# Score blocks of an attention unit set between the matmuls of an up tile, in an mLSTM attention and FP4 FFN kernel

## The chip, the cores and the metric

The kernel runs on one core of one Trainium2 chip. The metric is the device time in microseconds (us) of one execution, the median of several. Names of engines are those of the profile: PE is the matmul engine (TensorE), PEld its weight loads, DVE is VectorE, ACT is ScalarE, POOL is GpSimd, SP is the engine that issues the transfers.

## What is computed

Two residual layers over `x` of 8 x 256 x 512. The first is an mLSTM attention with 16 heads of 32 elements, whose queries are the normalised `x` and whose keys and values are `ctx`. The second is a gated FFN with FP4 weights, inner width 1408.

```python
qk = jnp.einsum('bhsd,bhtd->bhst', qh, kh) / jnp.sqrt(dh)      # heads of 32
C = qk * D                                                      # D: decay matrix, from the gates
Cn = C / (jnp.maximum(jnp.abs(C.sum(-1, keepdims=True)), jnp.exp(-max_log_D)) + EPS)
h = jnp.einsum('bhst,bhtd->bhsd', Cn, vh)                       # then normalised per head
...
gate_up = jnp.einsum('bsh,oh->bso', x, w_gu)                    # w_gu = FP4 value * scale of 128 inputs
h = jax.nn.silu(gate) * up
y = jnp.einsum('bsi,hi->bsh', h, w_down)
...
x = x + _L0_xattn_ref(_layernorm(x), ctx, ctx, ...)
x = x + _L0_ffn_ref(_layernorm(x), ...)
```

## The kernel before

**Tiling.** The batch is taken in four pairs of sequences (512 tokens). Each pair first goes through the attention and then through the FFN. The function `iteration(p, q, n)` runs the attention of pair p beside the FFN of pair q = p - 1, and prepares pair n = p + 1. So the program has five stages: attention of pair 0 alone; attention 1 beside FFN 0; attention 2 beside FFN 1; attention 3 beside FFN 2; FFN 3 alone. The change touches the three in the middle.

**The attention of a pair** is cut into 8 units `u`, each with four heads of one sequence. A sequence of 256 tokens is two blocks of 128. For a unit PE computes:

- the scores (`scores`, L883): eight f32 products of 32 x 128 by 32 x 128, four for the even heads (`hh` = 0) and four for the odd ones (`hh` = 1). Two of them, `half` 0 and 1, use different 32 rows of the array and stand side by side. An f32 matmul is two instructions (two passes) with a weight load each;
- the state sums (`state_sums`, L895), one f32 product over all 128 rows, which needs `vw` from POOL (L505). In the program they stand between the two calls of `scores`;
- the values (`values_up`, L943): eight f32 products of 33 columns, and at their end one product with the state (L948) that releases DVE's `later` (L1214) and ACT's `tok` (L671).

**The FFN of a pair** has 22 up tiles `h` of 128 outputs. Each is four groups `g` (128 inputs each, with a scale of their own), and a group is two f16 matmuls of 128 x 512 (`up_group`, L1013), parts 0 and 1. The four groups use four PSUM banks, `pf` 0 to 3. ACT takes groups 0 and 1 out of the bank (`ts`, L698), DVE groups 2 and 3 (L1296, L1300). An up tile's group g may begin when group g of the tile before has been taken out.

**The order on PE** is written out by hand. With u = 1 to 7 one round of two up tiles reads: the odd tile, with a value product in front of each of its eight matmuls (`values_up`), then the state product L948, then `scores` of the next unit for `hh` = 0, `state_sums`, `scores` for `hh` = 1, then the even tile's eight matmuls in a row (`ffn_up`). In the stage with FFN 0 all unit work stands two tiles later (`LATE`).

**The order on DVE** in that round: L1296 and L1300 of the even tile, (in the stage with FFN 0 also L1364, a piece of the down weights), `later` L1214, L1296 and L1300 of the odd tile, then the two `products` L1201 (they wait for `qk_done`, which the last score matmul raises), `state` L1206, `gate` L1309, `add_later` L1224, and again L1296 and L1300 of the even tile. An engine takes its instructions in order, so the even tile's L1296 and L1300 are queued behind the products of the unit.

**POOL** in that round: two sums L535, the product `hT` L540 (waits for DVE's gate), the two masks L494, the two `vw` L505.

Of the kernel before, what the change touches and what calls it, by code (L numbers as in the profile page):

```python
# [32 lines left out]
P = 128  # L33
B, S, E, NH = 8, 256, 512, 16
DH = E // NH
PAIRS = B // 2
TT = 2 * S // P
KT = E // P
# [10 lines left out]
BLKS = 2  # L49
# [16 lines left out]
SCORES = {h: u for u, h in enumerate(SCORES_AT)}  # L66
# [43 lines left out]
def xattn_ffn(nc, x, ctx, ctxT, w_gates, b_gates, ln_scale, gu_bytes, gu_scales, dn_bytes, dn_scales, out):  # L110
# [7 lines left out]
    with es:  # L118
# [22 lines left out]
        xT = sb("xT", [P, 2 * KT, TT * P])  # L141
# [55 lines left out]
        po = es.enter_context(nc.psum_tensor("po", [P, 512], F32))  # L197
# [8 lines left out]
        def slot(q, h):  # L206

            return h - LATE if q == 0 else h
# [9 lines left out]
        def bank_qk(p, u, half):  # L218
            return pf[:, 2 * half] if p == 0 and u % 2 else pq[:, 2 * half]
# [52 lines left out]
        qk_half = sem("qk_half")  # L272
# [539 lines left out]
        def _(pe):  # L812
# [42 lines left out]
                last = pe.transpose(bank_back(p)[:, 8 * DH:8 * DH + ROWS], lf[:, 0, P:S], ident[0:ROWS, 0:ROWS])  # L855
                last.then_inc(back_done, 1)

            def scores(p, q, u, hh):
                hg, b = u // 2, u % 2
                if p == 0 and u == 1 and hh == 0:  # L860

                    pe.wait_ge(floor_ready, 2)
                if p > 0 and u == 0 and hh == 0:

                    pe.wait_ge(floor_ready, 2 * p + 2)
                if hh == 0:
                    pe.wait_ge(xT_read, KT * p + hg + 1)
                    if p == 0:
                        if u > 1:
                            pe.wait_ge(prod_done, 2 * u - 2)  # L870
                    elif u > 0:
                        pe.wait_ge(prod_done, 2 * UNITS * p + 2 * u)
                    elif q is not None:
                        pe.wait_ge(t_ready, 4 * FT * q + 1)
                        pe.wait_ge(acc_ready, 4 * FT * q + 1)
                else:
                    pe.wait_ge(qk_half, UNITS * p + u + 1)
                for blk in range(BLKS):
                    t0 = b * S + blk * P
                    for half in range(2):  # L880
                        r = slice((2 * half + hh) * DH, (2 * half + hh + 1) * DH)
                        c = (blk * 2 + hh) * P
                        last = pe.matmul(bank_qk(p, u, half)[:, c:c + P], xT[r, KT + hg, t0:t0 + P],  # L883
                                         xT[r, hg, t0:t0 + P], start=True, stop=True)
                last.then_inc(qk_done if hh else qk_half, 1)

            def state_sums(p, q, u):

                hg, b = u // 2, u % 2
                pe.wait_ge(vw_ready, 2 * UNITS * p + 2 * u + 2)  # L890
                if u > 0:
                    pe.wait_ge(later_ready, UNITS * p + u)
                elif q is not None:
                    pe.wait_ge(t_ready, 4 * FT * q + 2)
                pe.matmul(pq[:, 1, 0:HG * (DH + 1)], ctx_sb[:, 2 * b, hg * P:(hg + 1) * P],  # L895
                          vw[:, u % 2].rearrange("q h d -> q (h d)"), start=True, stop=True
                          ).then_inc(st_done, 1)
# [28 lines left out]
            def values_up(p, q, u, h):  # L926
                hg, b = u // 2, u % 2
                if u == 0 and q is not None:
                    pe.wait_ge(acc_ready, 4 * FT * q + 2)
                if p == 0 and u < 2:  # L930
                    pe.wait_ge(v_ready, 2 * u + 2)
                elif u == 0:
                    pe.wait_ge(v_ready, TT * p + TT)
                if u > 0:
                    pe.wait_ge(o_read, UNITS * p + u)
                elif not (isinstance(p, int) and p == 0):
                    pe.wait_ge(o_read, UNITS * p)
                for k in range(2 * HG):
                    half, blk, hh = k // HG, k // 2 % 2, k % 2
                    if k % HG == 0:  # L940
                        pe.wait_ge(prod_done, 2 * UNITS * p + 2 * u + 1 + half)
                    col = (blk * HG + 2 * half + hh) * (DH + 1)
                    pe.matmul(po[:, col:col + DH + 1], dmat[:, u % 2, half, blk, hh],  # L943
                              v_sb[:, 2 * b + blk, hg * HG + 2 * half + hh], start=True, stop=True)
                    up_group(q, h, k // 2, k % 2)

                pe.wait_ge(state_ready, UNITS * p + u + 1)
                pe.matmul(pq[:, 1, HG * (DH + 1):2 * HG * (DH + 1)], xT[:, hg, b * S + P:(b + 1) * S],  # L948
                          state[:, u % 2].rearrange("q h d -> q (h d)"), start=True, stop=True
                          ).then_inc(pv_done, 1)  # L950
# [48 lines left out]
            def up_group(q, h, g, part):  # L999

                prev = behind(q, h)
                if part == 0:
                    if spare(q, h) and (prev < 0 or not spare(q, prev)):
                        pass
                    elif prev < 0 or spare(q, prev) != spare(q, h):

                        if q > 0:
                            pe.wait_ge(y_scaled, TT * (q - 1) + g + 1)
                    elif g < 2:
                        pe.wait_ge(t_ready, 4 * FT * q + 2 * prev + 1 + g)  # L1010
                    else:
                        pe.wait_ge(acc_ready, 4 * FT * q + 2 * prev - 1 + g)
                ins = pe.matmul(bank(q, h, g), gu_val[:, h // 2 + h % 2 * FT, g], yT[:, part, g],  # L1013
                                start=(part == 0), stop=(part == 1))
                if part == 1:
                    ins.then_inc(pu_done, 1)
# [26 lines left out]
            def keep_busy(count, dst=None):  # L1043

                words = ident[:].bitcast(F16)
                for _ in range(count):
                    pe.matmul(pf[:, 3] if dst is None else dst, words[:, 0:P], words.unsqueeze(1).to_broadcast([P, 2, 2 * P]),  # L1047
                              start=True, stop=True)

            def iteration(p, q, n):  # L1050
                for h in range(GU):
                    if q is not None:
                        if p is not None and slot(q, h - 1) in VALUES:
                            values_up(p, q, VALUES[slot(q, h - 1)], h)
                        else:
                            ffn_up(q, h)
                    if p is not None:

                        s = slot(q, h)
                        if q is None and s in VALUES and VALUES[s] + 1 < UNITS:  # L1060
                            scores(p, q, VALUES[s] + 1, 0)
                            if VALUES[s] == 0:
                                keep_busy(6, po[:])
                            else:
                                keep_busy(3)
                        if q is None and s in VALUES:
                            values(p, q, VALUES[s])
                            if q is None and VALUES[s] + 1 < UNITS:
                                scores(p, q, VALUES[s] + 1, 1)
                                state_sums(p, q, VALUES[s] + 1)  # L1070
                                keep_busy(6 if VALUES[s] == 0 else 3)
                        if s in SCORES and (q is not None or SCORES[s] == 0):
                            scores(p, q, SCORES[s], 0)
                            if q is None:
                                keep_busy(8, po[:])
                            state_sums(p, q, SCORES[s])
                            scores(p, q, SCORES[s], 1)
                if q is not None:
                    down(q, 0, range(FT))
                    down(q, 1, range(FT))  # L1080
                if n is not None:
                    if q is None:
                        keep_busy(16)
                    turn_x(n)
                    gate_sums(n)
                    if q is None:
                        keep_busy(36)
                if q is not None:
                    down(q, 2, range(FT))
                if p is not None:  # L1090
                    turn_y(p)
                if q is not None:
                    down(q, 3, range(FT - 3))
                if n is not None:
                    turn_back(n)
                if q is not None:
                    down(q, 3, range(FT - 3, FT))
# [387 lines left out]
```

## Time and profile before

| | us |
|---|---|
| median of 3 runs | 537.66 |
| the runs | 537.6 to 538.22 |
| time of the profiled execution | 538.07 |
| its span, first to last instruction | 536.4 |
| PE busy | 492.7 |
| DVE busy | 390.9 |
| POOL busy | 332.8 |
| ACT busy | 295.1 |

The span is what the trace covers, and 1.7 us of the execution lie around it. In the trace a line of several instructions of a kind is merged: its start is that of the first, its length reaches to the end of the last, and xN is their number. A matmul's end is modelled, so the distance from start to start is what a matmul costs in a row of them. The time in square brackets is how long the engine was idle ahead of the line, and what released it.

### The profile page before, as it was taken

How to read it: one execution, taken by the hardware profiler on the slowest of the kernel's cores; microseconds unless marked ns; L12 is line 12 of the kernel's file. 1: busy time of each engine (PE TensorE's matmuls, PEld its weight loads, DVE VectorE, ACT ScalarE, POOL GpSimd, SP SyncE). 2: the span in 40 equal slices, each digit the busy share in tenths (PEclk: the TensorE clock that was granted, in tenths of full speed). 3: DMA queues.
4: the chain of work that ended last, by engine and by line, in shares of the span. 5: the costliest groups of instructions: out<-in, count | busy, mean ns of one | idle time of the engine just before them, and what ended most of it. 6: DMA issues, size and time to landing. Idle time of an engine off the chain costs nothing.

```text
span 536.4 us, 8218 instructions
## 1 busy us (share of the span) xinstructions
PE 492.7 (92%) x2752; PEld 284.4 (53%) x2752; DVE 390.9 (73%) x691; ACT 295.1 (55%) x639; POOL 332.8 (62%) x371
## 2 busy tenths in 40 slices
PE   0989996899999899999999999999999989989996
PEld 0556773437777344567774445577764443323442
DVE  4976878978898988278878997478879754777301
ACT  0356854387877342688877334788863125765010
POOL 2064546188887764568887883678879644888401
PEclk9988997999999999999999999999999999999999
DMA  8964037074103200366015001671000010200001
GB/s 273 253 208 148 3 107 266 16 265 156 41 2 133 104 0 2 107 214 232 0 41 198 0 1 42 203 270 40 1 1 1 20 40 20 79 0 1 21 20 39
DMA packets 22235, 47.81 MB, mean 89 GB/s; under 512 B 1841, under 2 KB 8881, under 8 KB 21681
## 3 DMA queue, kind: packets, MB, share of 16 engines
q1 hardware_dynamic: 22192, 47.28, 25.7%
q8 instruction: 22, 0.36, 0.3%
q14 instruction: 21, 0.16, 0.1%
HBM read 37.31 MB, written 4.33 MB: 78 GB/s over the span
## 4 chain that ended last, share of the span: by engine, by line
PE 63%; DVE 16%; POOL 7%; issue 6%; ACT 5%; DMA 1%; DVEq 0%; POOLq 0%; ACTq 0%
PE pf L1028 26%; PE pf L1013 14%; PE pq L883 6%; PE po L943 4%; PE pq L895 3%; POOL dmat L494 3%; POOL hT L540 2%; PE pq L1013 2%; PE po L917 2%; PE pf L1047 2%; DVE ffn L1296 2%; DVE dmat L1201 2%; ACT dmat L664 2%; DVE th L1309 1%; PE pq L842 1%
## 5 line engine op out<-in xcount | busy, mean ns | idle before, releaser
L1013 PE MATMUL pf<-yT,gu_val 128*128 128x512 f16 x552 | 158.7, 381 | 5.6 <-DVE ffn L1300 2.4
L1028 PE MATMUL pf<-w_down,hT 128*128 128x512 f32 x352 | 154.0, 595 | 1.7 <-DVE w_down L1364 1.7
L535 POOL TENSOR_TENSOR ffn<-ffn,ts 128x512 f32<-128x512 f32 x88 | 118.2, 1346 | 28.0 <-DVE ffn L1300 21.1
L1028 PEld LDWEIGHTS pf<-w_down,hT 128*128 128x128 f32 x352 | 65.9, 190 | 83.7 <-issue 77.2
L698 ACT ACTIVATE ts<-pf,gu_scale 128x512 f32<-128x512 f32 x138 | 86.9, 682 | 17.1 <-PE pf L1013 15.9
L1013 PEld LDWEIGHTS pf<-yT,gu_val 128*128 128x128 f16 x552 | 62.7, 121 | 52.2 <-DVE ffn L1300 8.9
L664 ACT ACTIVATE dmat<-negm,aT 128x128 f32<-128x128 f32 x248 | 77.6, 393 | 0.5 <-DMA negm<-negm_dram 0.5
L943 PEld LDWEIGHTS po<-v_sb,dmat 128*128 128x128 f32 x384 | 66.2, 191 | 8.0
L540 POOL TENSOR_TENSOR hT<-ffn,th 128x512 f32<-128x512 f32 x44 | 57.7, 1316 | 19.9 <-DVE th L1309 19.9
L494 POOL TENSOR_SCALAR_AFFINE_SELECT dmat<-dmat 128x512 f32<-128x512 f32 x64 | 44.2, 706 | 27.1 <-ACT dmat L664 27.1
L1296 DVE SCALAR_TENSOR_TENSOR ffn<-pf,gu_scale,ts 128x512 f32<-128x512 f32 x69 | 51.4, 745 | 12.7 <-ACT ts L698 12.1
L1300 DVE SCALAR_TENSOR_TENSOR ffn<-pf,gu_scale,ffn 128x512 f32<-128x512 f32 x69 | 51.8, 751 | 9.0 <-PE pf L1013 1.4
L943 PE MATMUL po<-v_sb,dmat 128*128 128x33 f32 x384 | 58.4, 234 | 0.0
L716 ACT ACTIVATE th<-pf 128x512 f32<-128x512 f32 x16 | 9.5, 592 | 72.7 <-PE pf L1028 72.7
L546 POOL TENSOR_SCALAR ms<-ssq 128x1 f32<-128x1 f32 x16 | 4.2, 260 | 61.1 <-ACT th L716 60.6
L883 PE MATMUL pq<-xT 32*128 32x128 f32 x448 | 40.9, 301 | 0.0
L1201 DVE SCALAR_TENSOR_TENSOR dmat<-pq,dmat 128x512 f32<-128x512 f32 x56 | 36.1, 686 | 6.4 <-PE pq L883 6.2
L484 POOL TENSOR_TENSOR v_sb<-ctx_sb,vmean 128x512 f32<-128x512 f32 x16 | 16.8, 1079 | 29.8 <-DVE negm L1186 18.5
L883 PEld LDWEIGHTS pq<-xT 32*128 32x128 f32 x448 | 30.0, 189 | 9.4 <-issue 3.3
L1309 DVE SCALAR_TENSOR_TENSOR th<-th,ffn 128x512 f32<-128x512 f32 x44 | 34.1, 782 | 0.0
L1013 PE MATMUL pq<-yT,gu_val 128*128 128x512 f16 x114 | 30.2, 393 | 2.3 <-issue 2.1
L707 ACT ACTIVATE th<-ffn 128x512 f32<-128x512 f32 x44 | 27.5, 626 | 8.1 <-POOL ffn L535 8.1
(128 smaller groups left out, 678.7 us busy)
## 6 DMA issues: line engine op xcount, KB each, us to landing
negm<-negm_dram SPq DMA_DIRECT2D x31, 512.0 KB, 5.6
ffn<-in_x SPq DMA_DIRECT2D x4, 1024.0 KB, 6.7
xT<-in_ctx_T SPq DMA_DIRECT2D x16, 256.0 KB, 5.8
ctx_sb<-in_ctx SPq DMA_DIRECT2D x4, 1024.0 KB, 5.4
x_sb<-in_x SPq DMA_DIRECT2D x4, 1024.0 KB, 5.3
x_res<-x_sb SPq DMA_DIRECT2D x4, 1024.0 KB, 4.7
out<-x_res SPq DMA_DIRECT2D x16, 256.0 KB, 2.1
ts<-in_gate_up_bytes SPq DMA_DIRECT2D x4, 352.0 KB, 9.3
```

The costliest lines, as they stand in the source:

```text
L494: pool.affine_select(out=d, in_=d, compare_op=ALU.is_ge, fill=0.0, base=0, pattern=[[0, HG], [1, P]], channel_multiplier=-1).then_inc(mask ...
L535: pool.tensor_tensor(acc, acc, ts[:, h % TDEEP, 1], ALU.add).then_inc(tsum_ready, 1)
L540: pool.tensor_tensor(hT[:, j], ffn[:, 6 + j % 2], th[:, j % 2], ALU.mult).then_inc(h_ready, 1)
L664: last = act.activation(dmat[:, u % 2, half, c, hh], m[:, c * P:(c + 1) * P], ACT.Exp, bias=aT[:, c, bh:bh + 1])
L698: act.activation(ts[:, h % TDEEP, g], bank(q, h, g), ACT.Copy, scale=gu_scale[:, g * GU + o:g * GU + o + 1]).then_inc(t_ready, 1)
L883: last = pe.matmul(bank_qk(p, u, half)[:, c:c + P], xT[r, KT + hg, t0:t0 + P], xT[r, hg, t0:t0 + P], start=True, stop=True)
L943: pe.matmul(po[:, col:col + DH + 1], dmat[:, u % 2, half, blk, hh], v_sb[:, 2 * b + blk, hg * HG + 2 * half + hh], start=True, stop=True)
L1013: ins = pe.matmul(bank(q, h, g), gu_val[:, h // 2 + h % 2 * FT, g], yT[:, part, g], start=(part == 0), stop=(part == 1))
L1028: last = pe.matmul(pf[:, tt], hT[:, j, tt * P:(tt + 1) * P], w_down[:, j], start=(j == 0), stop=(j == FT - 1))
L1201: dve.scalar_tensor_tensor(d, bank_qk(p, u, half), float(DH) ** -0.5, d, ALU.mult, ALU.mult).then_inc(prod_done, 1)
L1296: dve.scalar_tensor_tensor(acc, bank(q, h, 2), gu_scale[:, 2 * GU + o:2 * GU + o + 1], ts[:, h % TDEEP, 0], ALU.mult, ALU.add).then_inc(ac ...
L1300: dve.scalar_tensor_tensor(acc, bank(q, h, 3), gu_scale[:, 3 * GU + o:3 * GU + o + 1], acc, ALU.mult, ALU.add).then_inc(acc_ready, 1)
```

## The change

`scores` is split into its waits (`scores_free`) and its blocks (`score_block`, L886), and a new function `scores_up` puts the blocks of a unit, the state sums and the even up tile into one order. In front of each of the first four matmuls of the tile (groups 0 and 1, both parts) stands one score block, that is two products side by side; the state sums stand in the middle. Groups 2 and 3 follow in a row. The matmuls, their operands, the banks and the semaphores are the same; the stage without FFN keeps its order.

```diff
+            def scores_up(p, q, u, h):
+
+                scores_free(p, q, u, 0)
+                for blk in range(BLKS):
+                    score_block(p, u, 0, blk)
+                    up_group(q, h, 0, blk)
+                state_sums(p, q, u)
+                scores_free(p, q, u, 1)
+                for blk in range(BLKS):
+                    score_block(p, u, 1, blk)
+                    up_group(q, h, 1, blk)
+                for g in range(2, KT):
+                    up_group(q, h, g, 0)
+                    up_group(q, h, g, 1)
...
                         if p is not None and slot(q, h - 1) in VALUES:
                             values_up(p, q, VALUES[slot(q, h - 1)], h)
+                        elif p is not None and slot(q, h - 1) in SCORES:
+                            scores_up(p, q, SCORES[slot(q, h - 1)], h)
                         else:
                             ffn_up(q, h)
...
-                        if s in SCORES and (q is not None or SCORES[s] == 0):
+                        if q is None and s in SCORES and SCORES[s] == 0:
                             scores(p, q, SCORES[s], 0)
-                            if q is None:
-                                keep_busy(8, po[:])
+                            keep_busy(8, po[:])
                             state_sums(p, q, SCORES[s])
                             scores(p, q, SCORES[s], 1)
```

The order of instructions on PE, in a unit with u from 1 to 7 beside the FFN. `pq<-xT` is a score product, `pq<-vw,ctx_sb` the state sums, `pf<-yT,gu_val` a matmul of the up tile. Before:

```order
180 L883 MATMUL pq<-xT 128x128 [waits prod_done,xT_read]
181 L883 MATMUL pq<-xT 128x128 x3
182 L895 MATMUL pq<-vw,ctx_sb 128x132 [waits later_ready,vw_ready]
183 L883 MATMUL pq<-xT 128x128 [waits qk_half]
184 L883 MATMUL pq<-xT 128x128 x3
185 L1013 MATMUL pf<-yT,gu_val 128x512 [waits t_ready]
186 L1013 MATMUL pf<-yT,gu_val 128x512
187 L1013 MATMUL pf<-yT,gu_val 128x512 [waits t_ready]
188 L1013 MATMUL pf<-yT,gu_val 128x512
189 L1013 MATMUL pf<-yT,gu_val 128x512 [waits acc_ready]
```

The same place after the change:

```order
182 L886 MATMUL pq<-xT 128x128 [waits prod_done,xT_read]
183 L886 MATMUL pq<-xT 128x128
184 L1037 MATMUL pf<-yT,gu_val 128x512 [waits t_ready]
185 L886 MATMUL pq<-xT 128x128 x2
186 L1037 MATMUL pf<-yT,gu_val 128x512
187 L919 MATMUL pq<-vw,ctx_sb 128x132 [waits later_ready,vw_ready]
188 L886 MATMUL pq<-xT 128x128 [waits qk_half]
189 L886 MATMUL pq<-xT 128x128
190 L1037 MATMUL pf<-yT,gu_val 128x512 [waits t_ready]
191 L886 MATMUL pq<-xT 128x128 x2
192 L1037 MATMUL pf<-yT,gu_val 128x512
193 L1037 MATMUL pf<-yT,gu_val 128x512 [waits acc_ready]
```

Four matmuls of the up tile moved in between the score products: two ahead of the state sums, one between the last two pairs of score products, one behind them.

The order on PE at the first unit (u = 0) of a stage, where the scores follow the second up tile and not a tile with values. Before:

```order
149 L1013 MATMUL pf<-yT,gu_val 128x512
150 L883 MATMUL pq<-xT 128x128 [waits t_ready,acc_ready,xT_read,floor_ready]
151 L883 MATMUL pq<-xT 128x128 x3
152 L895 MATMUL pq<-vw,ctx_sb 128x132 [waits t_ready,vw_ready]
153 L883 MATMUL pq<-xT 128x128 [waits qk_half]
154 L883 MATMUL pq<-xT 128x128 x3
155 L1013 MATMUL pf<-yT,gu_val 128x512 [waits t_ready]
```

The same place after the change:

```order
149 L1037 MATMUL pf<-yT,gu_val 128x512
150 L886 MATMUL pq<-xT 128x128 [waits t_ready,acc_ready,xT_read,floor_ready]
151 L886 MATMUL pq<-xT 128x128
152 L1037 MATMUL pf<-yT,gu_val 128x512 [waits t_ready]
153 L886 MATMUL pq<-xT 128x128 x2
154 L1037 MATMUL pf<-yT,gu_val 128x512
155 L919 MATMUL pq<-vw,ctx_sb 128x132 [waits t_ready,vw_ready]
156 L886 MATMUL pq<-xT 128x128 [waits qk_half]
```

The same matmuls moved here. The order on DVE, ACT, POOL and SP is that of before.

## Rows read from the trace of the kernel before

**Rows 1.** The page, section 2: granted clock in 40 slices, in tenths.

```profile
PEclk9988997999999999999999999999999999999999
```

**Rows 2.** Busy time by stretch: PE, PEld, DVE, ACT, POOL, clock, DMA, in stages 2, 3.

```profile
117.50:173.40 55.90, 54.34 (x418) 41.23 (x418) 49.40 (x86) 43.25 (x105) 47.00 (x54) 1.00 0.24 83
230.40:283.70 53.30, 53.30 (x414) 40.69 (x414) 42.17 (x77) 43.21 (x104) 41.78 (x53) 1.00 0.35 125
```

**Rows 3.** Timeline of PE in the third stage, one round: start, length, line, count.

```profile
256.59 0.38 PE L1013 MATMUL pf<-yT,gu_val 128*128 128x512 f16 x1
256.81 0.39 PE L948 MATMUL pq<-state,xT 128*128 128x132 f32 x2
257.13 0.71 PE L883 MATMUL pq<-xT 32*128 32x128 f32 x8
257.77 0.49 PE L895 MATMUL pq<-vw,ctx_sb 128*128 128x132 f32 x2
258.19 0.71 PE L883 MATMUL pq<-xT 32*128 32x128 f32 x8
258.84 1.90 PE L1013 MATMUL pf<-yT,gu_val 128*128 128x512 f16 x8
...
262.16 0.38 PE L1013 MATMUL pf<-yT,gu_val 128*128 128x512 f16 x1
...
262.94 0.39 PE L1013 MATMUL pf<-yT,gu_val 128*128 128x512 f16 x1
...
263.53 0.39 PE L948 MATMUL pq<-state,xT 128*128 128x132 f32 x2
```

**Rows 4.** Timeline of DVE in the same round.

```profile
257.24 0.30 DVE L1214 TENSOR_TENSOR later<-pq,decay 128x132 f32<-128x132 f32 x1 [1.07 <-PE pq L948]
...
258.30 0.75 DVE L1300 SCALAR_TENSOR_TENSOR ffn<-pf,gu_scale,ffn 128x512 f32<-128x512 f32 x1
259.06 1.29 DVE L1201 SCALAR_TENSOR_TENSOR dmat<-pq,dmat 128x512 f32<-128x512 f32 x2
...
262.13 0.75 DVE L1300 SCALAR_TENSOR_TENSOR ffn<-pf,gu_scale,ffn 128x512 f32<-128x512 f32 x1
```

**Rows 5.** PE timeline, windows so narrow that first and last score passes stand alone.

```profile
257.13 0.38 PE L883 MATMUL pq<-xT 32*128 32x128 f32 x2
...
257.56 0.28 PE L883 MATMUL pq<-xT 32*128 32x128 f32 x2
...
258.63 0.28 PE L883 MATMUL pq<-xT 32*128 32x128 f32 x2
258.84 0.39 PE L1013 MATMUL pf<-yT,gu_val 128*128 128x512 f16 x1
```

**Rows 6.** PE timeline, narrow window: f16 matmul, then score products (first unit, second stage).

```profile
117.17 0.38 PE L1013 MATMUL pf<-yT,gu_val 128*128 128x512 f16 x1
117.48 0.38 PE L883 MATMUL pq<-xT 32*128 32x128 f32 x2
```

**Rows 7.** PE timeline, first stage: score passes, then a filler matmul without a wait.

```profile
60.02 0.39 PE L883 MATMUL pf<-xT 32*128 32x128 f32 x4
60.34 0.60 PE L1047 MATMUL pf<-ident 128*128 128x512 f16 x2
```

**Rows 8.** Timeline of PE, second stage, one round.

```profile
138.00 0.39 PE L948 MATMUL pq<-state,xT 128*128 128x132 f32 x2
...
139.24 0.49 PE L895 MATMUL pq<-vw,ctx_sb 128*128 128x132 f32 x2 [0.21 <-POOL vw L505]
139.66 0.71 PE L883 MATMUL pq<-xT 32*128 32x128 f32 x8
145.00 0.39 PE L948 MATMUL pq<-state,xT 128*128 128x132 f32 x2
...
146.24 0.49 PE L895 MATMUL pq<-vw,ctx_sb 128*128 128x132 f32 x2 [0.21 <-POOL vw L505]
```

**Rows 9.** Timeline of DVE, then of POOL, in the same round.

```profile
140.53 1.29 DVE L1201 SCALAR_TENSOR_TENSOR dmat<-pq,dmat 128x512 f32<-128x512 f32 x2 [0.30 <-PE pq L883]
...
143.60 0.75 DVE L1300 SCALAR_TENSOR_TENSOR ffn<-pf,gu_scale,ffn 128x512 f32<-128x512 f32 x1
...
145.63 0.55 POOL L505 TENSOR_TENSOR vw<-v_sb,dmat 128x66 f32<-128x66 f32 x2
```

**Rows 10.** Timeline of DVE at the first unit of the fourth stage.

```profile
345.11 1.29 DVE L1201 SCALAR_TENSOR_TENSOR dmat<-pq,dmat 128x512 f32<-128x512 f32 x2 [0.31 <-PE pq L883]
...
347.72 0.75 DVE L1300 SCALAR_TENSOR_TENSOR ffn<-pf,gu_scale,ffn 128x512 f32<-128x512 f32 x1 [0.46 <-PE pf L1013]
```

More of the change, by code:

```diff
@@ L856, in turn_back, with scores_free @@
                 last.then_inc(back_done, 1)
-            def scores(p, q, u, hh):
-                hg, b = u // 2, u % 2
+            def scores_free(p, q, u, hh):
+                hg = u // 2
                 if p == 0 and u == 1 and hh == 0:
@@ L877, in scores, with score_block @@
                     pe.wait_ge(qk_half, UNITS * p + u + 1)
-                for blk in range(BLKS):
[L879 to L885, printed above, removed]
+            def score_block(p, u, hh, blk):
+                hg, b = u // 2, u % 2
+                t0 = b * S + blk * P
+                for half in range(2):
+                    r = slice((2 * half + hh) * DH, (2 * half + hh + 1) * DH)
+                    c = (blk * 2 + hh) * P
+                    last = pe.matmul(bank_qk(p, u, half)[:, c:c + P], xT[r, KT + hg, t0:t0 + P],
+                                     xT[r, hg, t0:t0 + P], start=True, stop=True)
+                if blk == BLKS - 1:
+                    last.then_inc(qk_done if hh else qk_half, 1)
+            def scores(p, q, u, hh):
+                scores_free(p, q, u, hh)
+                for blk in range(BLKS):
+                    score_block(p, u, hh, blk)
+            def scores_up(p, q, u, h):
[11 more added lines that the diff above has]
+                    up_group(q, h, g, 1)
             def state_sums(p, q, u):
```

## The prediction

> **What bounds the kernel now.** I read the granted clock first: from the second stage on it is full [rows 1], and it is 1.00, the 2.4 GHz level, in both stretches of units that I priced [rows 2]. Then the busy time by stretch: in the third stage PE is busy for all 53.30 us, in the second for 54.34 of 55.90 [rows 2]. That looks like a kernel bound by PE, and the change as one that can give PE something. But a busy PE is not a PE that streams, since a matmul that waits for its weights counts as busy. So I went to single starts.
>
> A round in the third stage, from one state product L948 to the next, is 263.53 - 256.81 = 6.72 us [rows 3]. Within it PE has a small hole: the matmuls of groups 2 and 3 of the odd tile start at 262.16 and 262.94, 0.78 apart, where 0.72 (two value products and two f16 matmuls) would do. The even tile's L1300 on DVE ends at 262.13 + 0.75 = 262.88 [rows 4], and the matmul that needs its bank starts 0.06 later. So a **loop through DVE** is already tight: L948 starts; 2.25 later the products start (259.06); 3.82 later L1300 of the even tile ends (262.88), with no idle time in between; 0.06 later PE goes on; 0.59 later L948 starts. 2.25 + 3.82 + 0.06 + 0.59 = 6.72, the whole round. What starts the products at 259.06? Two things at once: L1300 of the odd tile ends at 258.30 + 0.75 = 259.05, and the last pass of the scores starts at 258.63 [rows 5]. In the second stage, where DVE does wait for the scores, the products start at 140.53, and the last pass there starts 0.44 after 139.66 [rows 8, 9], so the scores' last start and DVE are 0.43 apart; 258.63 + 0.43 = 259.06. Both are just in time.
>
> In the second stage a round is 145.00 - 138.00 = 7.00 us [rows 8]. There PE waits for POOL's `vw` at the state sums (0.21 idle), and the loop runs state sums, scores, products, gate, hT, masks, vw: 146.24 - 139.24 = 7.00. The DVE loop is slack in that stage by 0.28.
>
> **The price of a switch between 32 rows and 128 rows.** This decides the case. The steps, start to start:
> - In a run of score passes: 257.13 to 257.56 is three steps, 0.43. The first passes last 0.38 and later ones 0.28 [rows 5], so the first waits 0.10 longer for its weights: the steps are 0.21, 0.11, 0.11.
> - Scores to f16: 258.63 to 258.84, 0.21 [rows 5]. The pass itself takes 0.11, so 0.10 is lost. It is not the semaphore wait on that matmul: in the first stage a filler matmul without any wait also starts 0.32 after two passes of 60.02, so 0.21 after the last [rows 7].
> - f16 to scores: 117.17 to 117.48, 0.31 [rows 6], against 0.22 from an f16 matmul to the full-row L948 [rows 3]; 0.09 is lost, and the score pass again lasts 0.38, so its weights were not loaded under the f16 matmul: a further 0.10.
> - L948 to scores: the scores start 0.32 after L948 and L948's second pass 0.11 after its first, so 0.21: 0.10 lost, and again a 0.38 pass. Scores to state sums is 0.21 (257.56 to 257.77) [rows 3, 5]; from there to the next scores it is 0.42, of which 0.21 is such a step, so the state sums' two passes are 0.21 apart where 0.11 would do.
>
> So each step into the 32-row form costs 0.20, and each step out 0.10 and its exposed load (0.01 for f16, 0.11 for f32).
>
> **The change on PE.** Before, a unit has four such switches. After, eight: L948 to scores, out and in around three f16 matmuls, out to the fourth, and in again behind the state sums; only the step from f16 to state sums is a cheap one. I count from the start of L948. Before: scores 0.32, last pass 1.82, first f16 2.03, group 2 of the even tile at 2.03 + 0.23 + 3 x 0.215 = 2.90. After: scores 0.32; second pass 0.53; f16 0.74; scores +0.32 = 1.06; 1.27; f16 1.48; state sums +0.23 = 1.71; second pass 1.82; scores 2.03; 2.24; f16 2.45; scores 2.77; last pass 2.98; f16 3.19; group 2 at 3.42. PE's own stream grows by 3.42 - 2.90 = **0.52** a unit, and the last pass of the scores moves from 1.82 to 2.98, **1.16** later: it now has three f16 matmuls ahead of it besides.
>
> **The change on DVE.** It issues nothing new, but its products wait for that last pass: they start at 2.98 + 0.43 = 3.41 and not at 2.25. Queued behind them are the state copy, the gate, the late sum, and L1296 and L1300 of the even tile, for which PE waits in the odd tile. The round becomes 3.41 + 3.82 + 0.06 + 0.59 = 7.88, 1.16 more than 6.72. PE's own stream would be 6.72 + 0.52 = 7.24 less its 0.06 hole, so PE is to stand idle for some 0.6 a round where the groups 2 and 3 of the odd tile want their banks.
>
> ACT and POOL: groups 0 and 1 of the even tile now end early and far apart, which ACT can only use; POOL's hT, masks and vw follow the gate and are done 5.71 after the products start (140.53 to 146.24), while PE reaches its next state sums 3.82 + 0.65 + 1.71 = 6.18 after them. So vw is no longer waited for, and I cost both at nothing; if that cover of 0.47 went, it would be a longer round still. No transfer is moved.
>
> **The sum.** Third and fourth stage: 7 rounds of 1.16. The first unit has no gate and no late sum behind its products, and there DVE waited 0.31 ahead of the products and again 0.46 for PE ahead of L1300 [rows 10]; with that slack DVE's part of the shift, 1.16 - 0.46 = 0.70 less what PE waits for it anyway, comes out near PE's own, and I take PE's 0.52. That gives 2 x (7 x 1.16 + 0.52) = 17.3 for the two stages. Second stage: the DVE loop there is 3.41 + 3.82 (140.53 to 143.60 + 0.75) + 0.65 (144.35 to 145.00) = 7.88 against 7.00, so 7 x 0.88, and 1.16 for the first unit, since DVE has the gate behind its products already: 7.3. The first and last stage are as they were. Together 24.6. On the profiled execution's 538.07 that is 562.7, on the median of 537.66 it is **562.2 us**.
>
> **Rules that speak for and against.** The row-to-full switch without a wait [rows 7] is dear by 0.10. The Trainium skill, TensorEngine Tiling (Array Packing), section Tiling Modes, says that a change of tiling mode drains the array, without a price; by it each of the added switches costs something, the sum stays as it is, and the trace agrees with 0.10. The Trainium skill, TensorE: Matmul & The Clock Gate, Part 2: What happens when you issue a matmul, says that weight loads are pulled ahead of running matmuls when they go to the background buffer. By that rule alone the score weights would come in under the f16 matmuls and the time would be that of rival 2; the trace disagrees, with 0.38 for the pass behind an f16 matmul [rows 6].
>
> **Rivals.**
> 1. *PE's stream alone.* If DVE catches up (its chain shortened by a different overlap, or PE's wait on L1300 not in the way), only 0.52 x 24 = 12.5 is paid: 550.2. Against it: the round of 6.72 closes through DVE to 0.01. Chance 0.12.
> 2. *The interleaving works as in the value tiles:* no drain, loads hidden. Then seven score passes of 0.11, three f16 matmuls of 0.22, L948 and the state sums of 0.22 each lie ahead of the scores' last pass: 0.77 + 0.66 + 0.44 = 1.87 against 1.82 before; PE's stream shrinks by about 0.7 (four switches and their loads), but DVE's loop sets the round and stays at 6.72 to 6.77. In the second stage the state sums to last pass is 0.88 against 0.86. So 0 to 24 x 0.05 = 1.2: 537.7 to 538.9, the case that is **not slower**. It decides when rows of 0.38 behind an f16 matmul become 0.28 and the 0.31 becomes 0.22. Chance 0.09, as [rows 6] show the opposite at just such a place. A version in which only the two loads behind f16 matmuls are hidden takes 0.2 from each 1.16: 24.6 - 24 x 0.2 = 19.8, 557.5; that lies within my forecast's own range.
> 3. *A further loop opens,* POOL's or ACT's: the first of the two products is done 3.41 + 0.65 = 4.06 after L948, and the value matmuls want it at 3.42 + 4 x 0.215 = 4.28 less a load of 0.1, a margin of about 0.1. With 0.2 a unit more it is 567; the same place is where a fall of the clock to its lower level would start, as PE now idles in each round (in the second stage it idled 0.21 a round and kept 1.00 [rows 2, 8]). Chance 0.07 above 567.
>
> **How the numbers follow.** The forecast, 555 to 567, has 0.72; rival 1 0.12, rival 2 0.09, rival 3 0.07. The range reaches down to rival 1, 549, and up to 567, and leaves out rivals 2 and 3. About 0.2% is what a measurement here can tell from no change, 1.1 us: rival 2 is mostly within it, so the chances are 0.02 faster, 0.08 same, 0.90 slower.
>
> **What would show it.** Right: rounds of about 7.9 in all three stages, score lines of x4 with length 0.5 and a first pass of 0.38, f16 to scores 0.31, the products L1201 idle by about 1.1 ahead of each and released by PE's score line, and PE's odd-tile matmuls waiting for L1300 and L1296. vw no longer in PE's waits. Rival 1: rounds of 7.2 with DVE idle. Rival 2: passes of 0.28 and rounds of 6.7. I am wrong as a whole if the switch costs less between single pairs than at the places where I read it.

## The result, and the profile after

The changed kernel took **562.24 us** (median of 4 runs, 561.86 to 564.24) against 537.94 for the kernel before beside it: 1.045 times as long, 95% interval 1.042 to 1.047. The forecast was 562.2, range 549 to 567. The profiled execution's span grew from 536.4 to 560.1 us.

The granted clock, section 2 of the page of after; nothing changed there in the stages with units [rows 1]:

```profile
PEclk9979997899999999999999999999999999999999
```

The page's section 5, groups of after: name, shapes, count, busy time and mean of one, then the idle time ahead and its main releaser.

```profile
L1226 DVE SCALAR_TENSOR_TENSOR dmat<-pq,dmat 128x512 f32<-128x512 f32 x56 | 36.1, 686 | 33.0 <-PE pq L886 33.0
...
L886 PE MATMUL pq<-xT 32*128 32x128 f32 x448 | 53.8, 323 | 0.0
```

DVE's products had 6.4 us of idle time ahead of them and now have 33.0, all put down to PE's scores. The score matmuls are as many as before and their mean grew from 301 to 323 ns: more of them are first passes, with the wait for weights in their length.

One round on PE in the third stage (timeline of after), the answer to [rows 3]:

```profile
267.25 0.39 PE L972 MATMUL pq<-state,xT 128*128 128x132 f32 x2
267.57 0.49 PE L886 MATMUL pq<-xT 32*128 32x128 f32 x4
267.99 0.39 PE L1037 MATMUL pf<-yT,gu_val 128*128 128x512 f16 x1
268.31 0.49 PE L886 MATMUL pq<-xT 32*128 32x128 f32 x4
268.73 0.39 PE L1037 MATMUL pf<-yT,gu_val 128*128 128x512 f16 x1
268.96 0.39 PE L919 MATMUL pq<-vw,ctx_sb 128*128 128x132 f32 x2
269.28 0.49 PE L886 MATMUL pq<-xT 32*128 32x128 f32 x4
269.70 0.39 PE L1037 MATMUL pf<-yT,gu_val 128*128 128x512 f16 x1
270.02 0.49 PE L886 MATMUL pq<-xT 32*128 32x128 f32 x4
270.44 1.25 PE L1037 MATMUL pf<-yT,gu_val 128*128 128x512 f16 x5
...
273.68 0.39 PE L1037 MATMUL pf<-yT,gu_val 128*128 128x512 f16 x1 [0.36 <-DVE ffn L1321]
...
275.13 0.39 PE L972 MATMUL pq<-state,xT 128*128 128x132 f32 x2
```

From L972 to L972 (L948 of before) it is 275.13 - 267.25 = 7.88 us. Where a score line stands next behind an f16 matmul, it starts 0.32 after it; the state sums start 0.23 after theirs. What follows a score line starts 0.42 after it. At 273.68 PE stands still for DVE. DVE in the same round, the answer to [rows 4]:

```profile
267.67 0.30 DVE L1239 TENSOR_TENSOR later<-pq,decay 128x132 f32<-128x132 f32 x1 [1.07 <-PE pq L972]
267.89 0.74 DVE L1321 SCALAR_TENSOR_TENSOR ffn<-pf,gu_scale,ts 128x512 f32<-128x512 f32 x1
...
268.73 0.75 DVE L1325 SCALAR_TENSOR_TENSOR ffn<-pf,gu_scale,ffn 128x512 f32<-128x512 f32 x1
...
270.66 1.29 DVE L1226 SCALAR_TENSOR_TENSOR dmat<-pq,dmat 128x512 f32<-128x512 f32 x2 [1.18 <-PE pq L886]
...
273.74 0.75 DVE L1325 SCALAR_TENSOR_TENSOR ffn<-pf,gu_scale,ffn 128x512 f32<-128x512 f32 x1
```

Products at 270.66, 3.41 after the state product; even tile's last accumulation done at 274.49, 3.83 after them; PE's next state product 0.64 later. The sum is 7.88.

**Where the time went,** from the starts of the matmuls in both traces:

| | before | after | difference |
|---|---|---|---|
| second stage: first scores to first state product | 6.44 | 7.48 | 1.04 |
| its seven rounds | 49.05 | 55.14 | 6.09 |
| third stage: the same | 6.32 | 6.88 | 0.56 |
| its seven rounds | 47.26 | 55.15 | 7.89 |
| fourth stage: the same | 6.32 | 7.10 | 0.78 |
| its seven rounds | 47.01 | 55.15 | 8.14 |
| last state product to first down matmul, three stages | 22.46 | 22.46 | 0.00 |

That is 24.5. The units of the second stage began 0.73 earlier in this execution of after (116.75 and 117.48), and 24.5 - 0.7 is the 23.7 between the spans within 0.1.

### The profile page after: what moved, and what is told of

Read it like the earlier page. It is cut to its first block, busy times and chain, and to the rows that moved or that the text cites. A ratio compares the mean times of both kernels' runs of the same rounds, so it can differ in the third digit from the quotient of the medians.

```text
span 560.1 us, 8218 instructions
## 1 busy us (share of the span) xinstructions
PE 511.2 (91%) x2752; PEld 288.2 (51%) x2752; DVE 390.7 (70%) x691; ACT 296.4 (53%) x639; POOL 332.0 (59%) x371
## 4 chain that ended last, share of the span: by engine, by line
PE 64%; DVE 17%; issue 8%; ACT 5%; POOL 4%; DMA 1%; DVEq 0%; POOLq 0%; ACTq 0%
PE pf L1052 25%; PE pf L1037 12%; PE pq L886 8%; DVE ffn L1321 4%; PE pf L1071 3%; DVE th L1334 3%; PE pq L842 2%; PE po L941 2%; PE po L967 2%; PE pq L1037 2%; PE pq L919 2%; DVE dmat L1226 1%; DVE tok L1249 1%; DVE ffn L1325 1%; ACT dmat L664 1%
## 5 line engine op out<-in xcount | busy, mean ns | idle before, releaser
L1037 PE MATMUL pf<-yT,gu_val 128*128 128x512 f16 x552 | 172.3, 383 | 13.5 <-DVE ffn L1321 8.4
L698 ACT ACTIVATE ts<-pf,gu_scale 128x512 f32<-128x512 f32 x138 | 89.8, 681 | 22.0 <-PE pf L1037 20.5
L1037 PEld LDWEIGHTS pf<-yT,gu_val 128*128 128x128 f16 x552 | 61.5, 119 | 64.0 <-DVE ffn L1321 15.0
L886 PE MATMUL pq<-xT 32*128 32x128 f32 x448 | 53.8, 323 | 0.0
L886 PEld LDWEIGHTS pq<-xT 32*128 32x128 f32 x448 | 33.7, 188 | 20.2 <-issue 14.2
L671 ACT ACTIVATE tok<-po 128x264 f32<-128x264 f32 x32 | 12.5, 390 | 44.5 <-PE pq L972 34.3
```

Source lines behind the costliest of these rows:

```text
L698: act.activation(ts[:, h % TDEEP, g], bank(q, h, g), ACT.Copy, scale=gu_scale[:, g * GU + o:g * GU + o + 1]).then_inc(t_ready, 1)
```

## The experiments

Each line of a diff is against the kernel that the text names; the label's expectation was written ahead of the run. The totals scatter by more than some of these edits are worth: the first stage, whose order is the same but for ACT's squares in the last three runs, ended (first scores of the second stage) anywhere from 115.4 to 119.8 us in the profiled executions. So what an edit costs is read from the rounds, and the totals stand beside them.

**Four switches, or eight.** The changed kernel with the four matmuls moved in twos:

```diff
-                scores_free(p, q, u, 0)
-                for blk in range(BLKS):
-                    score_block(p, u, 0, blk)
-                    up_group(q, h, 0, blk)
+                scores(p, q, u, 0)
+                up_group(q, h, 0, 0)
+                up_group(q, h, 0, 1)
                 state_sums(p, q, u)
...
+                scores(p, q, u, 1)
+                up_group(q, h, 1, 0)
+                up_group(q, h, 1, 1)
```

> The changed kernel with the same four matmuls of the even tile moved among the scores, but in twos: four score products, two matmuls, state sums, four score products, two matmuls. So a unit has four switches between 32 and 128 rows, as before the change, and not eight. My theory: PE's stream is 0.08 us a round shorter than before (the state sums' weights load under a matmul), but the scores' last pass stands 0.34 later, DVE's loop becomes 7.06: 14 rounds of 0.34 and a few tenths in the second stage, about 543 us. Rival (only PE's stream counts): 0.08 x 24 less than before, 536 us. Second rival (it is the moving of f16 matmuls among scores that costs, not the switch): near 562 us.

Measured: 544.46 us, 1.013 of before (1.009 to 1.018). Rounds were 7.05 in all three stages, 4.9 us more than before with the first units; the other 2.3 of the 7.2 between the spans lie ahead of the second stage. PE, then DVE, in one round of it:

```profile
253.53 0.39 PE L970 MATMUL pq<-state,xT 128*128 128x132 f32 x2
253.85 0.71 PE L886 MATMUL pq<-xT 32*128 32x128 f32 x8
254.50 0.60 PE L1035 MATMUL pf<-yT,gu_val 128*128 128x512 f16 x2
254.94 0.39 PE L917 MATMUL pq<-vw,ctx_sb 128*128 128x132 f32 x2
255.26 0.71 PE L886 MATMUL pq<-xT 32*128 32x128 f32 x8
...
259.14 0.39 PE L1035 MATMUL pf<-yT,gu_val 128*128 128x512 f16 x1 [0.19 <-DVE ffn L1319]
```

```profile
256.12 1.29 DVE L1224 SCALAR_TENSOR_TENSOR dmat<-pq,dmat 128x512 f32<-128x512 f32 x2 [0.36 <-PE pq L886]
```

The state sums' line is 0.39 long and no longer 0.49: I read that as its weights coming in under the f16 matmul. PE has no more switches than in the kernel before and this load less, and yet the round is 0.33 longer, because the products start 2.59 after the state product and not 2.25. So the delay of the last score pass costs by itself, without any added switch; and the same f16 matmuls among the scores cost 18 us less when they stand in twos.

**The switch alone.** The kernel before, with one small matmul added between the two blocks of each `scores` call, over 128 rows in one run and over 32 (`ident[0:DH]`) in the other:

```diff
+                if tile is not None:
+                    pe.wait_ge(t_ready, 4 * FT * q + 2 * (tile - 1) + 1)
                 for blk in range(BLKS):
+                    if blk == 1 and tile is not None:
+                        words = ident[0:P].bitcast(F16)
+                        pe.matmul(bank(q, tile, 0)[:, 0:DH], words[:, 0:P], words[:, 0:DH], start=True, stop=True)
                     t0 = b * S + blk * P
```

The added wait, for the bank that the small matmul writes, costs nothing: in both runs the scores start 0.32 after the state product, as in the kernel before.

> The kernel before, with one small f16 matmul over 128 rows and 32 columns added between the two score blocks of each call of the scores, two a unit, 48 in all; its result is overwritten. It adds switches and nothing else. My theory: 0.33 us for each, out 0.10, in 0.10, exposed score weights 0.10 and the matmul 0.03, so rounds of 6.72 + 0.66 = 7.38 and about 551.6 us. Rival (a switch costs nothing, the lost time is that of the f16 matmuls' length): 48 x 0.03 or less, 537 to 539 us.

> The same small matmul at the same 48 places, but over 32 rows, so that the array stays in its 32-row form. My theory: no switch, so only the matmul's own 0.03 to 0.06 us each, rounds of 6.8, 538 to 541 us. Rival (any foreign matmul between two score blocks costs, by its other type, bank or weights, whatever its rows): the same time as the one over 128 rows.

Measured: over 128 rows 551.97 us, 1.028 of before (1.022 to 1.033), rounds of 7.35; over 32 rows 540.33 us, 1.006 (1.004 to 1.008), rounds of 7.00, 6.82 and 6.82. PE in a unit of the 128-row run:

```profile
252.95 0.39 PE L953 MATMUL pq<-state,xT 128*128 128x132 f32 x2
253.27 0.49 PE L888 MATMUL pq<-xT 32*128 32x128 f32 x4
253.69 0.19 PE L883 MATMUL pf<-ident 128*128 128x32 f16 x1
253.81 0.49 PE L888 MATMUL pq<-xT 32*128 32x128 f32 x4
254.23 0.49 PE L900 MATMUL pq<-vw,ctx_sb 128*128 128x132 f32 x2
```

and of the 32-row run:

```profile
251.11 0.39 PE L953 MATMUL pq<-state,xT 128*128 128x132 f32 x2
251.43 0.49 PE L888 MATMUL pq<-xT 32*128 32x128 f32 x4
251.76 0.17 PE L883 MATMUL pf<-ident 32*128 32x32 f16 x1
251.76 0.48 PE L888 MATMUL pq<-xT 32*128 32x128 f32 x4
252.18 0.49 PE L900 MATMUL pq<-vw,ctx_sb 128*128 128x132 f32 x2
...
253.25 1.90 PE L1018 MATMUL pf<-yT,gu_val 128*128 128x512 f16 x8
```

From the first score line to the state sums is 0.96 in the one and 0.75 in the other, against 0.64 in the kernel before [rows 3]. The matmul over 128 rows costs 0.32, as added up from the steps; over 32 rows 0.11 here. The second small matmul of the unit, behind the state sums, costs nothing over 32 rows: from the state sums (252.18) to the first f16 matmul (253.25) it is 1.07, as in the kernel before [rows 3]. So the round grows by 0.10, from 6.72 to 6.82, and not by 0.22. Type, bank and weights are those of the same tile of numbers; the rows are what differs. With 32 rows the second stage kept its 7.00: there PE waits 0.21 for `vw` ahead of the state sums anyway, which takes up the 0.11, and the part behind them did not get longer.

**Is it PE's own stream or DVE's loop?** The changed kernel, with another order on DVE:

```diff
-                if u is not None:
-                    products(p, u, range(2))
-                    keep_state(p, u)
...
                         ffn_up(q, h, p, u)
+                        if h % 2 == 1 and h > 1:
+                            gate(q, h // 2 - 1)
+                        if u is not None:
+                            products(p, u, range(2))
+                        if p is not None and s in VALUES:
+                            keep_state(p, VALUES[s])
+                        if p is not None and s - 1 in ADD:
+                            add_later(p, ADD[s - 1])
                         if q == 0 and h % 2 == 0:
                             down_weights(h // 2)
-                        if h % 2 == 1 and h > 1:
-                            gate(q, h // 2 - 1)
...
-                    if p is not None and s in ADD:
+                    if q is None and s in ADD:
                         add_later(p, ADD[s])
```

> The changed kernel, with the DVE order of a round altered: the gate ahead of the two products, the state copy and the late sum behind the even tile's two accumulations. PE's order is that of the changed kernel. My theory (a round of 7.88 us closes through DVE: late last score pass, products, even tile's accumulations; PE's own stream is 7.24): DVE then needs 3.41 + 2.82 + 0.65 = 6.88 a round, so PE binds and rounds fall to about 7.24, in all 548 us. Rival (the added time is all PE's own, switches dearer than I priced them, and DVE only waits along): nothing changes, rounds of 7.88, 562 us.

Measured: 552.97 us, 1.029 of before (1.026 to 1.032). The rounds fell from 7.88 to 7.19 in all three stages, with PE's order untouched, so 0.69 of each was DVE's and not PE's. The total fell by 9 us only, not by 14: the ends of the stages, from the last state product to the first down matmul, grew from 6.28, 8.09 and 8.09 to 7.66, 9.88 and 9.87.

**What the same DVE order gives the kernel before.** With it alone, and with one f16 matmul between the first four score products and the state sums:

> The kernel before with the altered DVE order alone (gate ahead of the products, state copy and late sum behind the even tile's accumulations). My theory: in stages three and four the round of 6.72 us closes through DVE with a hole of 0.08 on PE, so PE's 6.64 becomes the round; in the second stage, where the loop ran over gate, hT, masks and vw, it falls from 7.00 to about 6.7. Together 3 to 3.5 us less, about 534.4 us. Rival (the kernel before is bound by PE): no change, 537.7 us.

> The altered DVE order, and one matmul of the even tile between the first four score products and the state sums, the other three behind the unit: four switches, the state sums' weights loaded under the matmul. My theory: PE's stream is 0.09 us a round shorter than in the kernel with the altered DVE order alone, 24 x 0.09 = 2.2 us, about 532.2 us. Rival (the state sums' second pass waits for something else than its weights): the time of the altered DVE order alone, or 0.2 us a unit more for a further delay of the scores.

Measured: 541.23 us, 1.005 (1.003 to 1.006), and 539.21 us, 1.001 (1.000 to 1.003). The rounds were as expected, 6.63 and 6.54, in all three stages (the last of the third excepted, 6.88 and 6.89); in the second stage alone the seven rounds of 6.63 are 2.6 us shorter than before. But both totals missed, by 7 us each. The stages' ends were 1.3, 1.8 and 1.7 us longer here too in the first of the two, and behind the second stage the clock was granted at its lower level for 3.4 us, which made the stretch from the first down matmul to the next scores 52.77 us and not 51.09. The end of the fourth stage in the first of the two:

```profile
404.25 0.95 DVE L1224 TENSOR_TENSOR tok<-tok,later 128x132 f32<-128x132 f32 x1
...
405.24 1.06 ACT L681 ACTIVATE dmat<-tok 128x1024 f32<-128x1024 f32 x1 [2.30 <-DVE tok L1224]
...
406.20 1.25 ACT L698 ACTIVATE ts<-pq,gu_scale 128x512 f32<-128x512 f32 x2
...
406.93 1.61 PE L1013 MATMUL pq<-yT,gu_val 128*128 128x512 f16 x6 [0.71 <-ACT ts L698]
```

ACT stands at its squares (L681) for 2.30 us, waiting for the late sum that my order had put later, and its copies of the next tile are queued behind, and PE behind those. I had costed the move of the late sum at nothing and had looked only at DVE.

**The late sum back in its place.** The two orders again with `add_later` straight behind the products:

> The kernel before with DVE's gate ahead of the two products and the state copy behind the even tile's accumulations; the late sum keeps its place. In the run before_dve_relieved the rounds were as short as expected (6.63), but ACT's squares at the end of a stage waited for the later late sum, and with them ACT's copies of the next tile. My theory: rounds of 6.63 again, the stages' ends as in the kernel before, so 14 x 0.09 + 7 x 0.37 = 3.8 us less, about 534 us. Rival (the lost time at the stages' ends comes from the gate or the state copy, or PE makes up for shorter rounds by waiting later): the 541 us of before_dve_relieved, or 537.7 us.

> The same DVE order, and one matmul of the even tile between the first four score products and the state sums (four switches a unit, the state sums' weights loaded under it). My theory: rounds of 6.54, stages' ends as before, 24 x 0.09 = 2.2 us less than gate_first, about 532 us, faster than both kernels of this case. Rival: the ends take it back as in one_matmul_between, 537 to 539 us.

> The changed kernel with the same DVE order. My theory: PE binds as in after_dve_relieved, rounds of 7.19, but the stages' ends stay at 6.3, 8.1 and 8.1 us as in the changed kernel, so 5 us less than the 553 us there: about 548 us. What is then left over the gate_first kernel, 14 us, is the price of the eight switches alone, 24 x 0.56. Rival: the ends are long because PE's rounds are shorter, 553 us.

Measured: 546.87 us, 1.014 (1.010 to 1.019); 543.50 us, 1.008 (1.005 to 1.011); 554.35 us, 1.029 (1.026 to 1.033), all slower than expected, by 13, 12 and 6 us. The ends were back at 6.28, 8.09 and 8.09, as expected, and the rounds were not: most took 7.52 and some 6.63 (6.54 in the second), 7.51 nearly throughout in the third. POOL and DVE in a round of 7.52 of the first:

```profile
404.74 1.27 POOL L540 TENSOR_TENSOR hT<-ffn,th 128x512 f32<-128x512 f32 x1
404.75 1.41 DVE L1224 TENSOR_TENSOR tok<-tok,later 128x132 f32<-128x132 f32 x1
```

The late sum, a sum of two operands in SBUF, takes 0.29 in a round of the kernel before and 1.41 here, started 0.01 behind POOL's hT; it ends 0.15 after hT. Of its 24 instances beside the FFN 21 took 1.36 to 1.41 us in this run, and 3 in the kernel before, all at a stage's end. The rounds of 6.63 are just those in which it took 0.28. The earlier gate had moved hT to just this moment. With the changed kernel's PE order (after_gate_first) the late sum started later within hT, took less, and again ended 0.15 after it:

```profile
266.98 1.28 POOL L540 TENSOR_TENSOR hT<-ffn,th 128x512 f32<-128x512 f32 x1
267.68 0.73 DVE L1249 TENSOR_TENSOR tok<-tok,later 128x132 f32<-128x132 f32 x1
```

The products there start 3.41 after the state product as in the changed kernel, so the longer late sum was enough to let DVE set the round again, 7.51 and not 7.19. The Trainium skill, SBUF — State Buffer, section SBUF: two separate sides, says that a VectorE operation with two SBUF inputs and a GpSimd operation that reads SBUF lock a shared port pair for their whole length and that the later one blocks; the trace agrees.

**Both mended.** The DVE order as in after_dve_relieved, with the late sum behind the accumulations, and ACT's squares one tile later:

```diff
-SQUARES = {SCORES_AT[-2] + 3: 0, SCORES_AT[-1] + 3: 1}
+SQUARES = {SCORES_AT[-2] + 4: 0, SCORES_AT[-1] + 4: 1}
```

> The kernel before_dve_relieved, with ACT's two squares at the end of a stage one tile later. There the rounds were 6.63 but ACT's copies of the next tile stood behind squares that waited for the late sum, 1.3 to 1.8 us a stage. In gate_first the late sum, put straight behind the products, took 1.40 us instead of 0.29 because POOL's hT had just started. My theory: the late sum takes 0.28 in the rounds, rounds of 6.63, the stages' ends 6.3 to 7.0, 8.1 to 8.9 and 8.1 to 8.9 us, about 535 us. Rival (the ends wait for DVE, not for ACT's squares): ends of 7.6, 9.9 and 9.8 us and 540 us again.

> The same with one matmul of the even tile between the first four score products and the state sums. My theory: rounds of 6.54, ends as in the kernel beside it, about 533 us, faster than both kernels of this case. Rival: 538 to 539 us, as one_matmul_between.

> The changed kernel's PE order with the same DVE and ACT order: PE binds, rounds of 7.19, and against the first kernel of this call only the eight switches a unit are left, 24 x 0.56 = 13.4 us more than that one, about 548 us. Rival (part of the change's cost is neither PE's switches nor DVE's wait): more than 15 us above that one.

Measured: 535.37 us, **0.994 of before** (0.992 to 0.996); 534.81 us, **0.993** (0.991 to 0.996); and with the changed kernel's PE order 548.66 us, 1.019 (1.015 to 1.022). Rounds 6.63, 6.54 and 7.19; ends of the third and fourth stage 7.9. DVE in a round of the first, for comparison with [rows 4]:

```profile
252.37 0.68 DVE L1306 SCALAR_TENSOR_TENSOR th<-th,ffn 128x512 f32<-128x512 f32 x1
252.97 1.28 DVE L1201 SCALAR_TENSOR_TENSOR dmat<-pq,dmat 128x512 f32<-128x512 f32 x2
...
255.02 0.75 DVE L1300 SCALAR_TENSOR_TENSOR ffn<-pf,gu_scale,ffn 128x512 f32<-128x512 f32 x1
...
255.89 0.29 DVE L1224 TENSOR_TENSOR tok<-tok,later 128x132 f32<-128x132 f32 x1
```

Two versions so beat both kernels, by 0.6 and 0.7% of the kernel before; between the two the intervals do not decide. The first and the third met what I expected (535 and 548), the second missed its 533 by 1.8. The second stage's end stayed 1.3 us long in them, with PE waiting there for DVE's last piece of the down weights, 2.45 us and not 1.66 as before. Behind that wait the clock was granted at its lower level for 3.4 us (PE's timeline and then the by-stretch view of the first of the three; the clock is the third number from the end of a row):

```profile
177.84 6.68 PE L1028 MATMUL pf<-w_down,hT 128*128 128x512 f32 x11 [2.45 <-DVE w_down L1361]
```

```profile
170.00:178.30 8.30, 4.93 (x23) 2.07 (x22) 8.05 (x10) 6.48 (x10) 4.83 (x4) 1.00 0.66 239
178.50:181.70 3.20, 3.20 (x5) 1.24 (x4) 3.15 (x4) 0.00 (x0) 2.25 (x2) 0.50 0.02 5
```

From the first down matmul to the next stage's scores is then 52.79 us and not 51.09. The third run had the same wait of 2.45 and kept the upper level there, with 51.09. It gives the price of the change with PE bound on both sides. In the two traces the 21 rounds take 151.05 us against 139.57 and the three first units 20.63 against 19.24: 12.9 us, which is 24 x 0.54, for four more switches a unit less the hidden load of the state sums' weights. The medians differ by 13.3 and the two spans by 10.4 only: the third run did not pay the 1.7 for the clock, and its first stage ended 0.9 earlier.

## Why the prediction was right

- **The switch between 32 and 128 rows.** Predicted steps after the change 0.32, 0.53, 0.74, 1.06, 1.48, 1.71, 2.03, 2.45, 2.77, 3.19 from the state product; in the trace the lines stand at 0.32, 0.74, 1.06, 1.48, 1.71, 2.03, 2.45, 2.77, 3.19 (0.53 is a pass inside a line). The added matmul of 128 rows cost 0.32 for 0.33. That it is the rows and not the foreign matmul is shown by the run with 32 rows. Why a switch costs 0.10 and keeps the next weights out was not looked into further than the lengths of the passes.
- **PE's own stream, 0.52 a unit.** In the runs in which DVE no longer binds the rounds are 6.63 and 7.19: 0.56. Group 2 of the even tile starts 0.52 later, as added up; the other 0.04 lies behind it and was not looked into.
- **The products 1.16 later, and the round closing through DVE at 7.88.** 3.41 and 7.88 in the trace. Shown from both sides: PE's order kept and DVE's changed gives 7.19; switches kept at four and the last pass delayed gives 7.05.
- **vw no longer waited for.** PE's wait for it is gone in the second stage, where DVE's loop now sets 7.88.
- **The sum.** 8.64 each were forecast for the fourth and the third stage and 7.3 for the second; 8.92, 8.45 and 7.13 came. That they add up to 24.5 for the forecast's 24.6 is luck in part, since the errors cancel: 0.3 too little in the fourth stage, 0.2 too much in each of the others; and the median came out at 562.2 among runs from 561.9 to 564.2. The term that was mis-sized most is the first unit of the fourth stage, where I took PE's 0.52 and 0.78 came. I had read the 0.46 ahead of L1300 as a wait for PE [rows 10]. It was no slack: the same 0.46 stands there after the change, with the products 1.16 later (the second row below, from DVE's timeline of after), though PE's last matmul of that tile had started at 361.77 and lasted 0.38, and the first unit of the third stage has no such wait in either kernel. So DVE set this round. The same 0.46 is found at the last unit of the third stage, in the kernel before at 278.80 (the first row below) and in the changed one at 292.72. Counted along DVE's instructions in the trace these are the 576th and the 704th, in both kernels. At the 576th there are 0.46 or 0.47 in all fourteen runs, whatever the order on PE; at the 704th in the five runs with the DVE order of before, and in none of the others. What holds DVE up at these places stays open. In the kernel before it had made the last round of the third stage 6.96; at 7.88 it is covered, so that this stage's rounds gained 0.24 back.

```profile
278.80 0.75 DVE L1300 SCALAR_TENSOR_TENSOR ffn<-pf,gu_scale,ffn 128x512 f32<-128x512 f32 x1 [0.46 <-DVE ffn L1296]
...
363.73 0.75 DVE L1325 SCALAR_TENSOR_TENSOR ffn<-pf,gu_scale,ffn 128x512 f32<-128x512 f32 x1 [0.46 <-PE pf L1037]
```

- **Rivals.** The stream alone (550.2) fell with the 7.88; the working interleave (537.7 to 538.9) fell with the steps of 0.32 and the first passes of 0.38 wherever a score line stands behind an f16 matmul. Of rival 3 nothing came: the round is the 7.88 that was added up, and the granted clock stayed at its upper level through the stages with units.

## What to carry to other kernels

Before a stalling engine is given filler, ask what form of the array the filler needs: here a step between 32-row and 128-row matmuls lost 0.10 us each way and kept the next f32 weights from being loaded ahead (0.10 more), so a filler of 0.22 us was paid for with 0.3. An engine that is busy for the whole of a stretch need not set its length; follow one round from a start to the same start over the engines, and see whether a second loop closes at the same number. Last, what an operation moved on one engine costs is found on the others: the late sum cost nothing in DVE's row, 2.3 us in ACT's queue at one place and 1.1 us against POOL at another.

## What the runs showed that I had not expected

The sum of two SBUF operands on DVE took 0.29 us, or up to 1.41 when it started just behind a POOL operation, and a round could settle in either: 6.63 or 7.52 us in one execution, by whether the two met. The totals of that kernel scattered from 542.7 to 549.9 us, where the kernel before, beside it, took 537.4 to 542.3; that the scatter comes of the number of such meetings is likely and not shown, as one execution was profiled. A small matmul in the 32-row form, between matmuls of that form, cost 0.11 us at one place and nothing at the other, and 0.10 in a round of two.
